# The causal mask of an attention score block: from four TensorE products into PSUM to four VectorE adds in PSUM

## What is computed

```
s_full = jnp.einsum('bnhd,bmhd->bhnm', q, k) * scale
causal = idx[:, None] >= idx[None, :]
slc_mask = blk_sel[..., idx // BS] & causal[None, None]
p_slc = jax.nn.softmax(jnp.where(slc_mask, s_full, -1e+30), axis=-1)
swa_mask = causal & (idx[:, None] - idx[None, :] <= WIN)
p_swa = jax.nn.softmax(jnp.where(swa_mask[None, None], s_full, -1e+30), axis=-1)
```

## Time and profile before

| what | value |
|---|---|
| median of 3 executions | 2504.64 us (2504.16 to 2505.31) |
| the profiled execution | 2504.16 us, of which the span is 2502.3 us |
| PE matmul busy | 2428.0 us (97%) |
| DVE busy | 1901.3 us (76%) |
| ACT busy | 1409.8 us (56%) |
| POOL busy | 1584.8 us (63%) |
| mean granted TensorE clock | 0.991 |

### The profile page before, as it was taken

How to read it: one execution, slowest core, us unless ns; L and a number is a source line. 1 busy time by engine, 2 the same in 40 slices (tenths; PEclk the granted TensorE clock), 3 DMA queues, 4 the chain that set the end, 5 groups by cost and what they waited for, 6 DMA issues and landing times. The chain is left out here.

```text
span 2502.3 us, 48659 instructions
## 1 busy us (share of the span) xinstructions
PE 2428.0 (97%) x12944; PEld 2066.0 (83%) x12944; DVE 1901.3 (76%) x5863; ACT 1409.8 (56%) x3808; POOL 1584.8 (63%) x1198
## 2 busy tenths in 40 slices
PE   6999999999999999999999999999978999999998
PEld 5788888888888888888888888888867888887776
DVE  7588888888888888888888888888882777775123
ACT  7566666666666666666666666666652222213442
POOL 1777777777777777777777777777753333333442
PEclk9999999999999999999999999999989999999999
DMA  4222212121222222222222222222225333432366
GB/s 153 60 71 55 75 50 75 50 75 50 75 63 63 63 63 63 62 64 62 64 71 54 71 54 71 54 71 54 58 72 188 133 115 121 155 110 76 102 180 215
DMA packets 145681, 211.78 MB, mean 85 GB/s; under 512 B 14960, under 2 KB 56176, under 8 KB 144624
## 3 DMA queue, kind: packets, MB, share of 16 engines
q1 hardware_dynamic: 145648, 211.37, 28.9%
HBM read 93.87 MB, written 50.33 MB: 58 GB/s over the span
## 5 line engine op out<-in xcount | busy, mean ns | idle before, releaser
L526 PE MATMUL bank<-xt_hi,w_hi 128*128 (+1 forms) x1536 | 619.3, 403 | 3.0 <-PEq L170 0.8
L526 PE MATMUL bank<-xt_hi,w_lo 128*128 (+1 forms) x1536 | 600.8, 391 | 0.0
L526 PE MATMUL bank<-xt_lo,w_hi 128*128 (+1 forms) x1536 | 598.1, 389 | 0.0
L501 POOL TENSOR_TENSOR qk_lo<-s_full,qk_hi 128x512 fp32r<-128x512 f32 x256 | 330.1, 1290 | 274.9 <-ACT qk_hi L621 274.9
L489 POOL TENSOR_TENSOR cosed<-s_full,rope 128x512 f32<-128x512 f32 x256 | 330.6, 1292 | 134.0 <-ACT s_full L610 130.6
L497 POOL TENSOR_TENSOR s_full<-cosed,s_swap 128x512 f32<-128x512 f32 x256 | 333.6, 1303 | 36.7
L526 PEld LDWEIGHTS bank<-xt_hi,w_lo 128*128 128x128 f32 x1536 | 288.2, 188 | 64.1
L526 PEld LDWEIGHTS bank<-xt_hi,w_hi 128*128 128x128 f32 x1536 | 289.2, 188 | 56.6 <-DVE w_lo L138 3.5
L526 PEld LDWEIGHTS bank<-xt_lo,w_hi 128*128 128x128 f32 x1536 | 289.5, 188 | 52.7
L494 POOL TENSOR_TENSOR s_swap<-s_swap,rope 128x512 f32<-128x512 f32 x256 | 332.9, 1300 | 0.1
L626 ACT ACTIVATE pt_hi<-bank 128x384 fp32r<-128x384 f32 (+1 forms) x384 | 174.7, 529 | 260.7 <-PE bank L568 260.5
(11 more groups left out here) (166 smaller groups left out, 5416.9 us busy)
## 6 DMA issues: line engine op xcount, KB each, us to landing
s_swap<-s_full SPq DMA_DIRECT2D x512, 128.0 KB, 2.3
o_scratch<-o_sb SPq DMA_DIRECT2D x128, 256.0 KB, 2.3
o_raw<-o_scratch SPq DMA_DIRECT2D x32, 1024.0 KB, 6.3
w_raw<-in_L_ffn_W SPq DMA_DIRECT2D x64, 256.0 KB, 3.1
xin<-in_L_attn_x SPq DMA_DIRECT2D x15, 1024.0 KB, 5.5
base_scratch<-x SPq DMA_DIRECT2D x8, 1024.0 KB, 4.7
base<-base_scratch SPq DMA_DIRECT2D x32, 256.0 KB, 4.3
out<-base SPq DMA_DIRECT2D x32, 256.0 KB, 3.3
```

Source lines behind the costliest of these rows:

```text
L501: nc.gpsimd.tensor_tensor(qk_lo[k][:], s_full[k][:], f32(qk_hi[k][:]), ALU.subtract).then_inc(lo_done[k], 1)
L526: last = nc.tensor.matmul(banks[QB[k]][:, :], w[k][:, c, :], v[:, bass.ds(b, 1), c, :], start=(n == 0), stop=(n == 3 * C - 1))
```

## The change

The four mask products go, with the two bf16 tiles they used and their casts. A score bank is now announced by its own third product. VectorE adds the mask, in fp32 from the constants, to the 128x128 diagonal block of a bank in place, and waits for that add by a semaphore of its own before it takes the row's minimum.

```
-    ident_h = r("ident_h", [P, P], BF16)
-    causal_h = r("causal_h", [P, P], BF16)
...
+    causal_masked = S("causal_masked")
...
-                            nc.tensor.matmul(banks[t][:, 0:w], x[:, t * P:(t + 1) * P], v[:, 0:w], start=(n == 0), stop=(n == 2),
-                                             skip_group_check=True)
-                    for t in SCORED:
-                        nc.tensor.matmul(banks[t][:, t * P:(t + 1) * P], ident_h[:], causal_h[:], start=False, stop=True,
-                                         skip_group_check=True).then_inc(scores_ready, 1)
+                            last = nc.tensor.matmul(banks[t][:, 0:w], x[:, t * P:(t + 1) * P], v[:, 0:w], start=(n == 0), stop=(n == 2),
+                                                    skip_group_check=True)
+                        last.then_inc(scores_ready, 1)
...
+                block = banks[t][:, t * P:(t + 1) * P]
                 dve.wait_ge(scores_ready, v * T + scored_at[t])
+                nc.vector.tensor_tensor(block, block, m("causal"), ALU.add).then_inc(causal_masked, 1)
+                dve.wait_ge(causal_masked, v * T + masked_at[t])
                 nc.vector.tensor_reduce(shift1[:, t:t + 1], n[:, 0:(t + 1) * P], AX.X, ALU.min)
...
-                    dve.wait_ge(scores_ready, v * T + scored_at[0])
                     read(v, 3)
...
-            nc.vector.memset(sc, 0.0).then_inc(zeros_set, 1)
-            nc.vector.tensor_copy(ident_h[:], m("ident")).then_inc(zeros_set, 1)
-            nc.vector.tensor_copy(causal_h[:], m("causal")).then_inc(zeros_set, 1)
+            nc.vector.memset(sc, 0.0).then_inc(zeros_set, 3)
```

## The result

| kernel | median | runs | ratio to the kernel before, 95% interval |
|---|---|---|---|
| before | 2504.64 us | 5 (2504.12 to 2509.36) | |
| changed | 2515.08 us | 5 (2514.71 to 2516.01) | 1.0038 (1.0024 to 1.0053) |
| changed, on another chip | 2515.45 us | 5 (2515.30 to 2517.52) | 1.0054 (1.0041 to 1.0068) |

The kernel before was timed on the other chip too (median 2503.62 us), and each ratio of an experiment is to the kernel before on the same chip. One execution on record enters no comparison: that of `e4_adds_apart_tile_moved` under the profiler took 4686.04 us at a mean granted clock of 0.940, where the four others of that kernel took 2488.74 to 2490.80.

The account below looks back on a forecast made before the run. TensorE was taken to bound attention, with VectorE taking over after the change. Ordinary steps +4.9, first steps +6.3 and second steps +14.7 sum to 25.9 us on 2504.16, giving 2530 us, range 2506 to 2556.

Parts of the forecast that it names:

- TensorE bounds the ordinary step before: In attention before the change, TensorE, busy 599.54 of 600 us, sets the pace of the 13.84 us step.
- VectorE's chain of 12.57 us: VectorE's own step without slack, read in two places, leaving a reserve of 1.27 us against 13.84.
- Price of an add, 0.33: Each 128x128 mask add on VectorE, with its self-wait, costs 0.33 us; four cost 1.32 a step.
- Ordinary steps, 13.89: In 97 steps VectorE's chain of 13.89 us overtakes TensorE's 13.61; each is 0.05 longer, together +4.9 us.
- First steps: First step of a head change, 15 times: middle of two bounds, +0.28 and +0.56, is +0.42 each, +6.3 us.
- Second steps: Second step of a head change, 15 times: quick and slow forms go from mean 14.12 to 15.10, +14.7 us.
- Start and end at nothing: The removed casts, and the last steps' earlier bank 3 against four adds, cost nothing, 1 us either way.
- From 1090.60 on they would not be held by it: TensorE's transposes wait for `v_lo`, which ends at 1090.47, so it would not hold them once the products go.
- The self-wait is hidden: Rival: an add costs only 0.21, VectorE's chain is 13.41, below TensorE's 13.61; 2488 us, chance 0.10.
- It cancels: Rival: at an add price of 0.27 to 0.29, ordinary steps win what head changes lose; 2504 us, chance 0.10.
- The dear add: Rival: each add costs 0.39, as the dearest row, 30.5 us over the forecast; 2560 us, chance 0.15.
- What would show it: Signs in the changed profile: exponentials wait about 0.75 us a step, ScalarE waiting for L766, TensorE idle 0.28 before transposes.

Follow-up runs that it names:

- e4_adds_apart_tile_moved: The changed kernel with each add one bank ahead of its read and the third weight tile's low half inside VectorE's wait for the exponentials: 2489.63 us, ratio 0.9956.
- e1_no_mask: The changed kernel with the four adds and their waits left out, so no causal mask is applied to the scores: 2485.76 us, ratio 0.9939.
- the adds apart: The changed kernel with each add put one bank ahead of its read: 2499.98 us, ratio 1.0000.
- e5_high_q_last: The kernel of e4_adds_apart_tile_moved with ScalarE making q's high half behind the exponentials of all banks: 2472.47 us, ratio 0.9882.

## Why the prediction was right and wrong

*TensorE bounds the ordinary step before.* Right: 13.83 with a shorter loop beside it.

*VectorE's chain of 12.57 us.* Right for the kernel before, wrong as what would be left of it in the changed one. 0.09 of it was the late sum, which went with the change. It was in both places from which I took the number, so their agreement did not show it.

*Price of an add, 0.33.* Right: duration 289 ns for 0.30, distance to the minimum 0.32, of which 0.12 is the self-wait. The sentence of the Trainium skill (VectorE: DVE Perf Modes, "The DRAIN you can't avoid"), by which "the semaphore costs nothing extra here", was measured there on `tensor_copy` and does not carry over to these operations: the adds apart show 0.20 against 0.32. The prediction also left out that the same section lets a next operation "that is not held" start earlier, and this is what the 0.20 shows: the minimum starts 0.09 before the add of 289 ns has ended.

*Ordinary steps, 13.89.* This is the step that failed: the term was +4.9 us and measured -3.0, which is 7.9 of the 15.0 us by which the sum of 25.9 missed the 10.9 between the spans. That VectorE takes over as the bound was right; the length of its chain was not. With the late sum gone it is 12.57 - 0.09 + 1.32 = 13.80, which is what was measured (13.81). Over 97 steps the 0.09 is 8.7 us, and it turns a small loss into a small gain. Where cost and reserve are both near 1.3 us, a tenth that hangs on the place of an instruction decides the sign.

*First steps.* +6.3 forecast, +7.5 measured. The middle between two bounds was not needed: the upper one, VectorE's chain, sets the step. Two errors in it nearly cancel. The tile displaced 0.98 (1070.49 to 1071.47) where I had 0.92, and the late sum is not in these steps in either kernel, so the chain is 12.48 + 0.98 + 1.32 = 14.78, which was measured.

*Second steps.* +14.7 forecast, +11.8 measured. The idea held that the two forms would merge into one between them, 12.48 + 1.11 + 1.32 = 14.91; the tile displaces 1.11 where I took about 1.2, and the late sum is gone here too.

*Start and end at nothing.* Attention is 16.3 us longer from the first to the last `v_lo`, exactly the three terms. Behind it 5.4 us were missing that the sum had put at nothing, a third of the miss. Two traces of each kernel show 4.0 to 5.4, no run shows why, and this part of the failure stays open.

*"From 1090.60 on they would not be held by it."* Wrong, and it was the worst reading, though it did not enter the sum. I compared the end of `v_lo` with the start of the transposes, and left out the 0.35 us that pass in an ordinary step between the two. With it there was no room: the transposes already started 1.05 after `v_lo` begins, and 1.03 is where a hold by `v_lo` shows in such a step. The 0.23 us of the mask products were not to be had by their removal alone; in `e1_no_mask` it gives 0.09, and by the same numbers 0.02 if the late sum had stayed.

*The rivals.* "The self-wait is hidden" would most likely not have given 2488 us even at its price: the kernel with the adds apart has 0.20 an add and takes 2500, since the loop through ScalarE stands at 13.75. "It cancels" came nearest to what happened in the ordinary steps, but by another way, and not at a price of 0.28. The dear add is excluded.

*What would show it.* VectorE's idle time ahead of the first minimum was gone, its wait was halved (0.68 us a step for 0.75), and ScalarE's wait for L766 and the steps of 14.5 to 15 were there. TensorE's gap ahead of the transposes is 0.31 from the last product's start, not an idle 0.28, because 0.12 of it is that product, and the view of the waits puts it down to "issue" and not to `v_lo`.

## The version that beats both

Adds one bank ahead of their reads, the third weight tile inside the wait for the exponentials, and q's high half behind them (`e5_high_q_last`): 2472.47 us, 1.2% less than the kernel before on that chip (2502.47), ratio 0.9882 (0.9865 to 0.9898). Its ordinary steps are bound by TensorE at 13.59 us. The adds apart alone give 2499.98 us, and q's high half moved in the kernel before 2492.42; the move of the tile was tried only on top of the adds apart.

## What to carry to other kernels

Moving work from the busiest engine to one that waits pays only up to the length of every loop that runs through both; here three loops (TensorE 13.84, TensorE and ScalarE and VectorE 13.75 or with the late sum 13.84, VectorE 12.57) stood so close that a saving of 0.23 gave 0.09 and an addition of 1.32 took the lead. Measure a loop by adding its hand-overs, not only its operations, and look for slack from start to start, at the place where the other engine really starts when it waits. An operation that waits for its own engine's last one should have something independent between them: it made each of the same four adds 0.12 us cheaper.

## What the runs showed of the hardware that I had not expected

- From the end of `v_lo` to the transposes that wait for it pass 0.35 us in every kernel where they are held, over ten times the 0.03 from VectorE to a waiting ScalarE (1108.07 to 1108.10, and in the 30 steps of the head changes of the changed kernel, in which ScalarE stood idle for 0.6) or to itself. In the first step of a head change the same transposes started 0.11 to 0.23 after `v_lo` ended, so not all of the 0.35 is the way from one engine to the other.
- The same wait of VectorE for ScalarE ended 0.19 or 0.10 us after ScalarE's row, depending on whether one unrelated one-column memset stood some twenty instructions ahead of it in the loop. Four memsets, and the four adds of the change, gave 0.10 as well, and within the kernel before it depends on the copy of the code that a step runs through.
- A weight tile of the same shape on VectorE took from 0.68 us (1053.09 above, while POOL stood idle from 1052.47 to 1054.74) to 1.49 with the adds apart and q's high half moved, and 1.81 in the kernel before, where POOL began an operation of 1.28 us at 1187.70, 0.02 ahead of it. That POOL's work is the cause was read from the timelines and not tested by itself.
